# The last quarter of each expert's down projection: from one float32 product to three float32r products

## The reference

```
gate_logits = xt @ Wg + bg;  top_v, top_i = top_k(gate_logits, 2)
... disp = tokens gathered into [8 experts, 80 slots, 512]
h   = silu(einsum('ecd,edh->ech', disp, W1)) * einsum('ecd,edh->ech', disp, W2)
out = einsum('ech,ehd->ecd', h, W3)
y   = sum over the token's two experts of softmax(top_v) * out[its slot]
```

## Time and profile before

| what | value |
|---|---|
| median of 3 runs | 1601.24 us (1597.68 to 1602.25) |
| the profiled execution | 1599.45 us |
| its span, first to last instruction | 1598.2 us |
| TensorE busy / VectorE / ScalarE | 1463.8 / 890.7 / 663.2 us |
| mean granted TensorE clock | 0.959 of full speed |
| first matmul of the first expert to the end of `down_full` of the last | about 1290.9 to 1591.07 us |

### The profile page before, as it was taken

How to read it: one execution, slowest core, us unless ns; L and a number is a source line. 1 busy time by engine, 2 the same in 40 slices (tenths; PEclk the granted TensorE clock), 3 DMA queues, 4 the chain that set the end, 5 groups by cost and what they waited for, 6 DMA issues and landing times.

```text
span 1598.2 us, 29598 instructions
## 1 busy us (share of the span) xinstructions
PE 1463.8 (92%) x12644; PEld 1121.2 (70%) x12644; DVE 890.7 (56%) x1312; ACT 663.2 (41%) x1207; POOL 247.8 (16%) x169
## 2 busy tenths in 40 slices
PE   7699999999999999999988885995986799999998
PEld 3379888887877878788876674882475476666665
DVE  3632433544445445554355535437867488888886
ACT  1424433433333443334444542431421246666664
POOL 1213211111020101201012232402061000000000
PEclk9989999999999999999999997997988789999999
DMA  7013101101010101101011228006000049999992
GB/s 249 2 44 96 57 30 40 44 21 41 27 39 21 44 24 41 41 21 44 21 44 41 82 81 316 16 0 237 0 3 27 1 146 343 346 345 342 343 338 86
DMA packets 86784, 163.22 MB, mean 102 GB/s; under 512 B 4608, under 2 KB 27136, under 8 KB 86144
## 3 DMA queue, kind: packets, MB, share of 16 engines
q1 hardware_dynamic: 86656, 161.34, 29.2%
HBM read 160.28 MB, written 1.05 MB: 101 GB/s over the span
## 4 chain that ended last, share of the span: by engine, by line
PE 86%; DVE 9%; issue 2%; ACT 1%; POOL 1%; DMA 0%; ACTq 0%; DVEq 0%
PE ring L591 18%; PE ring L581 16%; PE ring L1829 8%; PE turnbank L625 6%; PE pv L1853 4%; PE sc L608 3%; PE pv L644 3%; PE sc L1477 3%; PE sc L1065 3%; PE pv L1829 3%; PE pv L1861 2%; PE ring L1074 1%; PE pv L653 1%; DVE nm L813 1%; PE sc L348 1%
## 5 line engine op out<-in xcount | busy, mean ns | idle before, releaser
L549 POOL TENSOR_TENSOR x_l<-raw,x_h 128x1536 fp32r<-128x1536 f32 (+1 forms) x44 | 159.0, 3615 | 739.6 <-ACT x_h L543 739.6
L1678 DVE TENSOR_TENSOR w_lo<-w_raw,w_hi 128x2048 fp32r<-128x2048 f32 x88 | 200.4, 2285 | 25.3 <-ACT w_hi L1919 25.3
L731 ACT ACTIVATE prob<-sc,nm 128x384 f32<-128x384 f32 (+1 forms) x256 | 153.9, 611 | 118.9 <-DVE nm L818 80.1
L581 PE MATMUL ring<-x_h,wk_h 128*128 128x384 f32 (+1 forms) x512 | 186.4, 364 | 5.4 <-POOL x_l L549 5.4
L591 PE MATMUL ring<-wv_h,x_h 128*128 128x512 f32 (+2 forms) x520 | 190.9, 367 | 0.0
L813 DVE TENSOR_REDUCE nm<-sc 128x2 f32<-128x898 f32 (+1 forms) x128 | 128.0, 1020 | 104.5 <-PE sc L608 104.4
L591 PE MATMUL ring<-wv_h,x_l 128*128 128x512 f32 (+2 forms) x520 | 181.0, 348 | 0.0
L591 PE MATMUL ring<-wv_l,x_h 128*128 128x512 f32 (+2 forms) x520 | 180.7, 348 | 0.0
L581 PE MATMUL ring<-x_h,wk_l 128*128 128x384 f32 (+1 forms) x512 | 177.2, 346 | 0.0
L581 PE MATMUL ring<-x_l,wk_h 128*128 128x384 f32 (+1 forms) x512 | 176.6, 345 | 0.0
L1919 ACT CAST w_hi<-w_raw 128x2048 fp32r<-128x2048 f32 x88 | 167.6, 1907 | 18.4 <-PE pv L1853 15.5
(11 more groups left out here) (442 smaller groups left out, 2549.2 us busy)
## 6 DMA issues: line engine op xcount, KB each, us to landing
w_raw<-in_ew SPq DMA_DIRECT2D x96, 1024.0 KB, 5.3
raw<-in_ctxT SPq DMA_DIRECT2D x33, 768.0 KB, 4.4
raw<-in_ctxT SPq DMA_DIRECT2D x11, 900.0 KB, 4.7
wf<-in_wf SPq DMA_DIRECT2D x2, 4096.0 KB, 19.1
xin<-in_x SPq DMA_DIRECT2D x1, 1024.0 KB, 5.6
w_in<-in_wq SPq DMA_DIRECT2D x1, 1024.0 KB, 7.8
w_in<-in_wk SPq DMA_DIRECT2D x1, 1024.0 KB, 9.9
w_in<-in_wv SPq DMA_DIRECT2D x1, 1024.0 KB, 12.1
```

The costliest lines, as they stand in the source:

```text
L549: pool.tensor_tensor(x_l[x % 3][:, :, 0:w], raw[x % 3][:, :, 0:w], x_h[x % 2][:, :, 0:w].bitcast(F32), ALU.subtract)\
L581: m = pe.matmul(ring[k % 2][:, 0:w], wt[:, c, e:e + P], xt[:, c, 0:w], start=c == 0 and n == 0, stop=c == NC - 1 and n == 2)
L731: act.activation(prob[:, i, 0:WIDTHS[r]], sc[:, i, score_columns(r)], ACT.Exp, bias=nm[:, b % 2, r, h:h + 1], accum_out=psum[:, b % 2, r, ...
L1678: return eng.tensor_tensor(w_lo[n % NSLOT][:, :, :], w_raw[n % NSLOT][:, :, :], w_hi[i % 4][:, :, :].bitcast(F32), ALU.subtract)
```

## The change

The twelfth piece is split like the other eleven, and block 3 of the hidden units too. `SPLIT` and `splits_before` go; the split index is the piece number. `down_full` becomes `down(e, 3)`: twelve float32r matmuls, with the waits of the others. `hT_h` and `hT_l` have sixteen columns of tiles, `hT_f` is gone. The down part of ScalarE and VectorE has a fourth rounding and a fourth `dve_low` (q = 3), and VectorE has `turned_low` of block 3, placed behind the `dve_low` of q = 1.

```diff
-            for q in range(FB - 1):
-                dve_low(dve, splits_before(NPIECE * e + 2 * FB + q) + 4)
+            for q in range(FB):
+                dve_low(dve, NPIECE * e + 2 * FB + q + 4)
+                if q == 1:
+                    turned_low(FB * e + FB - 1)
             dve.wait_ge(sem("eout_high"), e + 1)
...
-            elif s % FB == 0:
-                pe.wait_ge(sem("hT_high"), s)
             else:
-                pe.wait_ge(sem("hT_low"), (FB - 1) * (s // FB) + s % FB)
+                pe.wait_ge(sem("hT_low"), s)
...
             if q == 0:
                 pe.wait_ge(sem("hidden_ready"), FB * e + 3)
-            pe.wait_ge(sem("hT_low"), (FB - 1) * e + q + 1)
+            pe.wait_ge(sem("hT_low"), FB * e + q + 1)
             piece_ready(n)
...
-        def down_full(e):
-            n = NPIECE * (e + 1) - 1
-            pe.wait_ge(sem("hT_high"), FB * (e + 1))
-            pe.wait_ge(sem(f"piece_loaded{n % NSLOT}"), 16 * (n // NSLOT + 1))
-            for f in range(4):
-                k = pe.matmul(down_bank[0:CAP, :], hT_f[:, f, :], w_raw[n % NSLOT][:, f, :], start=False, stop=f == 3)
...
             down(e, 2)
-            down_full(e)
+            down(e, 3)
...
-        if i < len(SPLIT):
-            n = SPLIT[i]
+        if i < NPALL:
+            n = i
             act.wait_ge(sem(f"piece_loaded{n % NSLOT}"), 16 * (n // NSLOT + 1))
             if i >= 4:
-                act.wait_ge(sem("pieces_used"), SPLIT[i - 4] + 1)
+                act.wait_ge(sem("pieces_used"), i - 3)
...
-            for q in range(FB - 1):
-                act_high(act, splits_before(NPIECE * e + 2 * FB + q) + 4)
+            for q in range(FB):
+                act_high(act, NPIECE * e + 2 * FB + q + 4)
                 if q == 1:
                     turned_high(FB * e + FB - 1)
             act.wait_ge(sem("pieces_used"), NPIECE * (e + 1))
```

More of the change, by code:

```diff
@@ L1622, in build @@
     disp_l = at("disp_l", R + 131072, [P, NC, NEXP * CAP], F32R)
-    hT_h = at("hT_h", R + 141312, [P, NH - 4, CAP], F32R)
-    hT_l = at("hT_l", R + 192512, [P, NH - 4, CAP], F32R)
-    hT_f = at("hT_f", R + 145152, [P, 4, CAP])
+    hT_h = at("hT_h", R + 141312, [P, NH, CAP], F32R)
+    hT_l = at("hT_l", R + 192512, [P, NH, CAP], F32R)
     counting = at("counting", R + 192512, [P, CAP], U32)
@@ L1647, in build @@
     y_bank, h_bank, down_bank = bank[0:4], bank[6], bank[7]
-    SPLIT = [n for n in range(NPALL) if n % NPIECE < NPIECE - 1]
     def expand_bank(fb, up):
         return (bank[4], bank[5], bank[7])[(2 * fb + up) % 3]
-    def splits_before(n):
-        return n - n // NPIECE
     def sp_experts(sp):
@@ L1750, in dve_experts @@
                 s, n = FB * e + fb, NPIECE * e + 2 * fb
-                i = splits_before(n)
+                i = n
                 dve.wait_ge(sem("hidden_tanh"), s + 1)
@@ L1825, in expand @@
             piece_ready(n)
-            out, tok, hi = expand_bank(fb, up), slice(e * CAP, (e + 1) * CAP), w_hi[splits_before(n) % 4]
+            out, tok, hi = expand_bank(fb, up), slice(e * CAP, (e + 1) * CAP), w_hi[n % 4]
             for c in range(NC):
@@ L1847, in down @@
                 pe.wait_ge(sem("hidden_ready"), FB * e + 3)
-            pe.wait_ge(sem("hT_low"), (FB - 1) * e + q + 1)
+            pe.wait_ge(sem("hT_low"), FB * e + q + 1)
             piece_ready(n)
-            hi = w_hi[splits_before(n) % 4]
+            hi = w_hi[n % 4]
             for f in range(4):
                 for i, (ht, wt) in enumerate(((hT_h, hi), (hT_h, w_lo[n % NSLOT]), (hT_l, hi))):
-                    k = pe.matmul(down_bank[0:CAP, :], ht[:, 4 * q + f, :], wt[:, f, :], start=q == 0 and f == 0 and i == 0, stop=False)
-            k.then_inc(sem("pieces_used"), 1)
-        def down_full(e):
-            n = NPIECE * (e + 1) - 1
-            pe.wait_ge(sem("hT_high"), FB * (e + 1))
-            pe.wait_ge(sem(f"piece_loaded{n % NSLOT}"), 16 * (n // NSLOT + 1))
-            for f in range(4):
-                k = pe.matmul(down_bank[0:CAP, :], hT_f[:, f, :], w_raw[n % NSLOT][:, f, :], start=False, stop=f == 3)
+                    k = pe.matmul(down_bank[0:CAP, :], ht[:, 4 * q + f, :], wt[:, f, :], start=q == 0 and f == 0 and i == 0,
+                                  stop=q == FB - 1 and f == 3 and i == 2)
             k.then_inc(sem("pieces_used"), 1)
@@ L1941, in turned_high @@
             f = slice(4 * (s % FB), 4 * (s % FB) + 4)
-            dst = hT_f[:, :, :] if s % FB == FB - 1 else hT_h[:, f, :]
-            act.copy(dst.rearrange("p f s -> p (f s)"), h_bank[:, 0:4 * CAP]).then_inc(sem("hT_high"), 1)
+            act.copy(hT_h[:, f, :].rearrange("p f s -> p (f s)"), h_bank[:, 0:4 * CAP]).then_inc(sem("hT_high"), 1)
         for e in range(NEXP):
```

## The result

The changed kernel takes 1610.32 us (median of 6 runs, 1609.05 to 1612.46) against 1601.74 us before (6 runs, 1597.66 to 1603.39). The ratio is 1.0062, with a 95% interval of 1.0045 to 1.0078: slower by 8.6 us. The forecast was 8.5 us slower.

A forecast was written before the change was run, and what follows sets the result against it. TensorE was taken to bound the expert stage. Seven experts at +1.31 us and the last at -0.67 gave +8.5 us: 1608.0 from the profiled execution, 1609.7 from the median; forecast 1609, range 1603.5 to 1614.

The forecast's parts named there:

- The product: TensorE, down part: `down_full` at 3.43 us becomes twelve float32r matmuls at 2.76 us, saving 0.67 us per expert.
- The stop: TensorE before piece 11 waits 1.88 us for `turned_low` of block 3, plus 0.10 us restart, in seven experts.
- The last expert has no stop: Down part of the last expert: `turned_low` ready 1.4 us after piece 9, covered by 3.04 us of TensorE work.
- VectorE late but in step again: VectorE, start of the next expert: 0.28 us late, in step again by the middle of the expert.
- rival C: TensorE at `expand(1, 0)` waits for `eout_l`, 0.3 us margin used up: 3.5 us added, 1612 to 1613; chance 0.08.
- Totals are no bound: VectorE needs 33.5 us per expert, below TensorE's 36.1 us, so its total is not the bound.
- rival D: TensorE's clock falls at every stop, 1.5 us each in seven experts: 10 us added, 1619; chance 0.04.
- What should show: New profile: seven TensorE waits for `hT_l` of about 1.9 us, experts about 38.1 us, clock 1.00, DMA share about 0.93.

The follow-up runs named there:

- Without the wait: Changed kernel, but piece 11 waits for `turned_high` only and its third product uses `hT_h` instead of `hT_l`: 1596.45 us, ratio 0.9969.
- the kernel with the two swaps: Changed kernel with block 3's `turned_low` (VectorE) and `turned_high` (ScalarE) ahead of the `dve_low` and rounding of q = 1: 1595.49 us, again 1595.92 us.
- the longer stop: Changed kernel with `turned_low` of block 3 behind the `dve_low` of q = 2 instead of q = 1: 1644.74 us, ratio 1.0267.
- The kernel with `eout` earlier: The kernel with the two swaps, with `eout_h` and `eout_l` ahead of the fourth rounding and fourth `dve_low`: 1595.76 us, ratio 0.9961.
- the one with `eout_l` later: The kernel with the two swaps, with `eout_l` behind the first gating of the next expert: 1598.66 us, ratio 0.9985.

## Why the prediction was right

**The product: 0.67 us less in each expert, 5.4 us in all.** Right. Without the wait the stage is 5.46 us shorter. The 230 ns of the row are what counted. The figure of the Trainium skill (TensorE: Matmul & The Clock Gate, Back-to-back issue gap), 216 ns, would have given 6.7 us; the section calls it the gap of an isolated matmul and says that in a stream of weight loads and matmuls it over-counts at large N. Here it under-counts: twelve of these matmuls take 2.72 to 2.80 us in the experts behind the first, 227 to 233 ns each. The last expert alone saved 0.53 us only (1601.43 - 1565.16 = 36.27 against 36.80 us), because the rest of its work took about 0.15 us longer than in the profile before.

**The stop: 1.88 us and a restart of 0.10.** Right, and in sum closer than its parts. It measured 1.91 and 0.06. The handover from VectorE took 0.05 to 0.06 us and not 0.04; the row that the 0.04 was read from says 0.05 itself (1592.56 to 1592.61). The restart was read from matmuls of another shape (80 rows, at 1592.61) and was cheaper here. That the two errors nearly cancel is luck. 7 x 1.97 = 13.8 us, and 14.1 us when it was put into the old kernel by itself.

**The last expert has no stop.** Right: seven waits, 36.24 us for the eighth window.

**VectorE late but in step again.** Right to 0.01 us, as the four starts above show. At 1429.11 VectorE again starts a gating for which it idled, 0.11 us behind the end of the operation ahead of it, where it was 0.23 us at 1423.52.

**No second stop at `eout_l`** (rival C). Right: no such wait is in the list, moving `eout_l` earlier gains nothing, and moving it later brings the stop.

**Totals are no bound.** Right. VectorE works 33.9 of 37.99 us in the changed kernel, and still the kernel with the two swaps runs a middle expert in 36.0 to 36.4 us with the same 33.9 us of work on it.

**The clock stays up** (rival D). Right for this kernel; the rows of the two earlier idle stretches had told the short from the long. In the longer stop the loss was 2.0 us each on average and not the 1.5 worked out from the row.

**What should show.** The DMA share is 0.91 to 0.92 (0.93 was said), the new gap of VectorE ahead of the last `dve_low` 2.45 us (about 2 was said), the experts 38.0 to 38.4 us (38.1) with TensorE busy 36.25 to 36.63 us of them (36.1), the last expert 36.24 us (36.0). `eout_h` starts 1.90 us after the end of the last piece (2).

**The number.** The sum gave +8.5 us and the medians say +8.6, the stage +8.9. The forecast of 1609 stands between the two totals that the prediction worked out, 1608.0 and 1609.7; the run-to-run spread of the base (1597.66 to 1603.39) is larger than the distance to 1610.32, so that closeness says little. What says more is that the two terms hold by themselves.

What the prediction didn't say, and might have: the stop comes from where the new step stands in the queue, and not from the work that the change adds. Putting `turned_high` and `turned_low` of block 3 ahead of the two splitting steps of q = 1 makes the same change 5.4 us faster than the old kernel, 0.3%, instead of 8.6 us slower.

## What to carry to other kernels

When an operation goes onto an engine with a queue in order, ask what stands ahead of it there and what that waits for. Here the order of two instructions of 0.4 and 2.2 us on VectorE took the stage from +8.9 to -4.3 us, and the same swap on ScalarE took away the last short wait. The engine's total load was the same in all three. Where the old trace already shows the instruction behind which the new one will stand, the stop can be read off it to a few hundredths.

When comparing two instants, take both from the same view: a margin of 0.15 us was gone because one was a modelled end and the other a start.

## What the runs showed of the hardware

**A long stop costs a second time.** After each of seven waits of about 4.8 us TensorE did about half of the next piece or all of it at half clock (matmuls of 512 columns 0.43 us apart instead of 0.23), which took 4.31 to 5.41 us instead of 2.99 and cost 2.0 us a time on average. Waits of 1.74 us, seven in a row with 36 us of work between them, left the clock at 1.00. The waits looked at here leave out the lengths between 1.98 us (clock kept) and 3.40 us (clock fell), so what decides in between isn't shown.

**The clock can fall while TensorE counts as busy.** In the first expert, behind 32 matmuls of two columns (2.23 us) that make `wslot`, eight of the ten profiles show a lower clock, and the two of the kernel with both swaps alone don't. The windows from 1300 to 1305 us, before and with both swaps (its second run):

```profile
1300.00:1305.00 5.00, 5.00 (x23) 3.21 (x23) 4.16 (x5) 0.25 (x1) 0.00 (x0) 0.68 0.25 95
```

```profile
1300.00:1305.00 5.00, 5.00 (x40) 3.82 (x40) 3.20 (x5) 1.48 (x2) 0.00 (x0) 1.00 0.45 172
```

Pieces 2 and 3 of the first expert take 4.10 + 3.08 us in the one and 2.85 + 2.79 in the other: 1.54 us. That is the 1.6 us by which the stage of the kernel with two swaps was shorter than expected. The kernel with `eout` earlier, with the same swaps, has 4.35 + 2.86 us there and a stage of 294.56 us, 1.57 us longer; the one with `eout_l` later, with the same swaps too, has 4.08 + 3.11 us there. Up to this point all these kernels issue the same instructions on TensorE, so the swap is not likely to be the cause. What decides it, and whether the short matmuls are what lowers the clock, I haven't tried.
